# Attention scores from two float32r parts on opposite halves of the array, in place of three bfloat16 parts on one

## What is computed

```python
xn = layernorm(x)                                  # x: 1024 x 512
q = rope(xn @ wq + bq)                             # 32 heads of 16
k = rope(xn @ wk + bk); v = xn @ wv + bv           # 8 key/value heads, each used by 4 heads
s = softmax(q @ k.T / sqrt(16)) @ v                # per head, 1024 x 1024 scores
z = xn @ W.T + b; m = sum_e p[e] * (xn @ A[e]) @ B[e]
g = silu(z + minimum(0.5 * norm(z) / (norm(m) + 1e-6), 1) * m)
out = x + s * g
```

## Time and profile before

| what | value |
|---|---|
| median of 3 runs | 495.08 us (494.57 to 496.36) |
| span of the profiled execution, first to last instruction | 494.9 us |
| opening part, to the first transposed scores | 104.2 us |
| groups 1 to 6, each | 47.34 us |
| TensorE / VectorE / ScalarE / GpSimd busy | 477.9 / 373.0 / 308.8 / 92.2 us |

### The profile page before, as it was taken

How to read it: one execution, slowest core, us unless ns; L and a number is a source line. 1 busy time by engine, 2 the same in 40 slices (tenths; PEclk the granted TensorE clock), 3 DMA queues, 4 the chain that set the end, 5 groups by cost and what they waited for, 6 DMA issues and landing times.

```text
span 494.9 us, 8174 instructions
## 1 busy us (share of the span) xinstructions
PE 477.9 (97%) x2437; PEld 166.2 (34%) x2437; DVE 373.0 (75%) x401; ACT 308.8 (62%) x603; POOL 92.2 (19%) x160
## 2 busy tenths in 40 slices
PE   7995999999999999999999999999999999999994
PEld 3772444432333332333232323232333323333231
DVE  5643898989888888888888888888888888833433
ACT  2221112377767777767777776767676777766774
POOL 4573225550000010001000100010001001001553
PEclk9997999999999999999999999999999999999999
DMA  8899965550000000000000000000000000002010
GB/s 302 263 119 117 116 79 64 64 66 1 2 0 3 2 1 1 1 0 1 0 1 0 1 0 1 0 1 0 1 0 1 0 1 1 0 2 75 19 49 29
DMA packets 16980, 17.06 MB, mean 34 GB/s; under 512 B 3394, under 2 KB 14914, under 8 KB 16962
## 3 DMA queue, kind: packets, MB, share of 16 engines
q1 hardware_dynamic: 15332, 15.21, 18.3%
q10 hardware_dynamic: 1632, 1.64, 1.0%
HBM read 6.76 MB, written 2.10 MB: 18 GB/s over the span
## 4 chain that ended last, share of the span: by engine, by line
PE 83%; DVE 4%; DMA 4%; POOL 3%; ACT 2%; issue 2%; SPq 1%; DVEq 0%
PE oT L839 26%; PE sm L777 24%; PE st L875 23%; PE sm L857 3%; DMA kA<-arena 2%; PE oT L720 2%; PE st L720 2%; DMA x_sb<-in_x 1%; PE sm L848 1%; POOL arena L315 1%; ACT arena L526 1%; DVE arena L577 1%; DVE arena L575 1%; DVE arena L573 1%; PE sm L860 1%
## 5 line engine op out<-in xcount | busy, mean ns | idle before, releaser
L595 DVE TENSOR_REDUCE negmax<-sm 128x1 f32<-128x1024 f32 x256 | 303.8, 1220 | 63.0 <-PE sm L777 62.4
L526 ACT ACTIVATE arena<-st 128x512 f32<-128x512 f32 x512 | 268.1, 601 | 99.0 <-PE st L875 98.2
L777 PE MATMUL sm<-kA,qA 96*128 (+1 forms) x512 | 155.1, 384 | 7.0 <-DMA kA<-arena 5.3
L875 PE MATMUL st<-qA,kA 98*128 (+1 forms) x512 | 158.4, 380 | 1.6 <-ACT arena L526 1.4
L839 PE MATMUL oT<-arena,vg 128*32 128x512 f32 x1024 | 136.4, 605 | 0.7 <-ACT arena L526 0.7
L777 PEld LDWEIGHTS sm<-kA,qA 96*128 (+1 forms) x512 | 39.5, 97 | 149.0 <-issue 117.8
L875 PEld LDWEIGHTS st<-qA,kA 98*128 (+1 forms) x512 | 49.1, 97 | 92.2 <-ACT arena L526 41.4
L361 POOL TENSOR_TENSOR maxp<-negmax,consts 128x16 bf16<-128x16 f32 x16 | 3.4, 215 | 261.9 <-PE st L875 210.6
L839 PEld LDWEIGHTS oT<-arena,vg 128*32 128x32 f32 x1024 | 20.1, 108 | 37.2 <-issue 24.8
L451 ACT ACTIVATE arena<-arena 128x512 bf16<-128x512 f32 x10 | 6.3, 630 | 40.8 <-POOL arena L315 40.8
L674 DVE TENSOR_TENSOR xT_sb<-sm,b_sb 128x512 f32<-128x512 f32 x4 | 2.8, 692 | 21.1 <-PE sm L860 21.1
(11 more groups left out here) (88 smaller groups left out, 255.0 us busy)
## 6 DMA issues: line engine op xcount, KB each, us to landing
qA<-arena SPq DMA_DIRECT2D x48, 128.0 KB, 5.4
x_sb<-in_x SPq DMA_DIRECT2D x8, 256.0 KB, 6.5
kA<-arena SPq DMA_DIRECT2D x12, 128.0 KB, 6.6
wT_sb<-in_wT SPq DMA_DIRECT2D x1, 1024.0 KB, 8.0
out<-x_sb SPq DMA_DIRECT2D x1, 896.0 KB, 4.0
out<-x_sb SPq DMA_DIRECT2D x4, 224.0 KB, 2.0
arena<-in_wq SPq DMA_DIRECT2D x1, 768.0 KB, 11.1
arena<-in_cosT ACTq DMA_DIRECT2D x1, 512.0 KB, 7.4
```

Of the source, the lines that this page charges most:

```text
L526: act.activation(probs[:, s % PB, h, :], st[:, (st_score(0, s, h) - late) % 3, :], ACT.Exp, scale=float(D) ** -0.5).then_inc(st_free, 1)
L595: dve.tensor_reduce(negmax[:, half, r:r + 1], sm[:, bank, :], AX.X, ALU.max, negate=True).then_inc(sm_free, 1)
L777: mm = pe.matmul(sm[:, bank, kh * HALF:(kh + 1) * HALF], qA[0:KR, half, bass.ds(g, 1), h, qt * P:(qt + 1) * P] .rearrange("p a n -> p (a n)"),
L875: pe.matmul(st[:, (st_score(0, s, h) - fewer) % 3, :], kA[:, bass.ds(g, 1), kt * P:(kt + 1) * P].rearrange("p a n -> p (a n)"), qA[:, half ...
```

## The change

q and k are split into two float32r parts (a high part, and what is left), three products of 16 rows: 48 partitions, 50 with the maxima. Even groups use partitions 0 to 49, odd groups 64 to 113 of `qA` and `kA`, which are now four-byte tiles. So row scores of group g+1 and transposed scores of group g lie in opposite halves of the array's rows, and `step` issues them in turn. Values moved behind the second of four pairs; in the last group the late pieces stand together behind the values. `turn_heads` stands ahead of the slot's first transposed scores. To put even and odd groups 64 partitions apart, the columns of wq (GpSimd, `put_columns`, from a landing place in `z_sb`), of wk (TensorE, every other column, two matmuls of 64 output rows) and the rows of the rope tables and biases (DMAs by halves, `load_tables`) are laid out anew. The rows of ones are a memset of all of `kA` on GpSimd instead of a DMA. Row entries of group 0 come two at a time behind every second matmul of a projection. TensorE's and SP's loops over groups are unrolled. Cut to its core:

```diff
-PARTS = 3
-Q_SLOTS = (0, 1, 0, 1, 0, 2)
-K_SLOTS = (0, 0, 1, 1, 2, 0)
+PARTS, PART_BUFS = 2, 3
+Q_SLOTS = (0, 0, 1)
+K_SLOTS = (0, 1, 0)
+ROWS = 64
+SLOT_DMAS = 2 * len(Q_SLOTS)
-PARTNER = [i ^ 8 for i in range(32)]
+PARTNER = [i ^ 4 for i in range(32)]
...
-        qA = sb("qA", [KM, 2, KV, REP, HALF], BF16)
-        kA = sb("kA", [KM, KV, S], BF16)
+        qA = sb("qA", [P, 2, KV // 2, REP, HALF], F32R)
+        kA = sb("kA", [P, KV // 2, S], F32R)
-        maxT = sb("maxT", [32, 2, P], BF16)
+        maxT = sb("maxT", [32, 2, P], F32R)
...
+        wq_came = z_sb[:, :, :].rearrange("p c (k d a h) -> p k a c d h", k=CHUNKS, a=2, h=REP)
+        wq_rows = wq_sb.rearrange("p c (k a d h) -> p k a c d h", k=CHUNKS, a=2, h=REP)
...
+        def load_tables(queue, odd):
-            sp.dma_start(wq_sb[:, :, P:E], wq_v[:, :, P:E]).then_inc(wq_in, 16)
+            load_tables(sp, 1)
+            sp.dma_start(z_sb[:, :, P:E], wq_v[:, :, P:E]).then_inc(wq_in, 16)
-            sp.dma_start(kA[KR:KM, :, :], ones).then_inc(ones_in, 16)
+            load_tables(act, 0)
...
                     maxima_row(0, 0)
                 of_slot = K_SLOTS if kind == "k" else Q_SLOTS
+                    sp.wait_ge((part1, part2)[of_slot[slot]], n + 1)
+                    for odd in range(2):
...
+                        sp.dma_start(to.bitcast(F32),
+                                     parts[odd * ROWS:(odd + 1) * ROWS, n % PART_BUFS, of_slot[slot], :]
+                                     ).then_inc(stacked[n], 16)
...
+            pool.memset(kA[:, :, :].bitcast(F32), 1.0).then_inc(ones_set, 1)
             pool.wait_ge(const_set, 6)
+
+            def put_columns(k):
+                for odd in range(2):
+                    pool.tensor_copy(wq_rows[:, k, odd], wq_came[:, k, odd]).then_inc(wq_put, 1)
 
             for t in range(NT):
                 pool.wait_ge(mean_var, t + 1)
                 pool.tensor_scalar(mv[:, t, 1:2], mv[:, t, 1:2], EPS_LN, None, ALU.add).then_inc(eps_added, 1)
                 pool.wait_ge(eps_added, t + 1)
                 pool.tensor_tensor(rstd[:, t:t + 1], mv[:, t, 1:2], consts[:, 0:1], ALU.pow).then_inc(rstd_done, 1)
+                if t == TH:
+                    pool.wait_ge(wq0_in, 16)
+                    put_columns(0)
+            pool.wait_ge(wq_in, 16)
+            for k in range(1, CHUNKS):
+                put_columns(k)
...
-            def left_over(n):
+            def low_part(n):
                 pool.wait_ge(part1, n + 1)
-                pool.tensor_tensor(rot[:, n % 2, :], rot[:, n % 2, :], parts[:, n % 3, 0, :],
-                                   ALU.subtract).then_inc(left1, 1)
-
-            def third_part(n):
-                pool.wait_ge(part2, n + 1)
-                pool.tensor_tensor(parts[:, n % 3, 2, :], rot[:, n % 2, :], parts[:, n % 3, 1, :],
-                                   ALU.subtract).then_inc(part3, 1)
+                pool.tensor_tensor(parts[:, n % PART_BUFS, 1, :].bitcast(F32R), rot[:, n % 2, :],
+                                   parts[:, n % PART_BUFS, 0, :], ALU.subtract).then_inc(part2, 1)
...
-                    if c < rows:
-                        next_maximum()
+                    if c % 2 == 1:
+                        for _ in range(max(0, min(2, rows - (c - 1)))):
+                            next_maximum()
...
+                            for odd in range(2):
+                                mm = pe.matmul(pj(n)[odd * ROWS:(odd + 1) * ROWS, tok], wk_sb[:, c, odd::2],
+                                               xT[:, i, c, tok], start=(c == 0), stop=(c == NE - 1))
...
-                if freed is not None:
-                    pe.wait_ge(sm_free, freed)
-                for kh in range(2):
+                rows = slice(ROWS * (g % 2), ROWS * (g % 2) + KR)
+                for kh in halves_of_keys:
+                    if kh == 0 and freed is not None:
+                        pe.wait_ge(sm_free, freed)
                     mm = pe.matmul(sm[:, bank, kh * HALF:(kh + 1) * HALF],
-                                   qA[0:KR, half, bass.ds(g, 1), h, qt * P:(qt + 1) * P]
-                                   .rearrange("p a n -> p (a n)"),
-                                   kA[0:KR, bass.ds(g, 1), kh * HALF:(kh + 1) * HALF].rearrange("p a n -> p (a n)"),
-                                   start=True, stop=True)
-                mm.then_inc(sm_full, 1)
+                                   qA[rows, half, g // 2, h, qt * P:(qt + 1) * P],
+                                   kA[rows, g // 2, kh * HALF:(kh + 1) * HALF], start=True, stop=True)
+                    if kh == 1:
+                        mm.then_inc(sm_full, 1)
...
                         pe.matmul(st[:, (st_score(0, s, h) - fewer) % 3, :],
-                                  kA[:, bass.ds(g, 1), kt * P:(kt + 1) * P].rearrange("p a n -> p (a n)"),
-                                  qA[:, half, bass.ds(g, 1), h, :].rearrange("p a n -> p (a n)"),
+                                  kA[rows, g // 2, kt * P:(kt + 1) * P], qA[rows, half, g // 2, h, :],
                                   start=True, stop=True).then_inc(st_full, 1)
 
-                    def next_rows(e):
+                    def next_rows(e, kh):
                         if not last:
                             n = sm_score(g, e, first)
-                            score_rows(g + 1, e, n, sm_score(0, e, first) % 2, n - 1)
+                            score_rows(g + 1, e, sm_score(0, e, first) % 2, n - 1, (kh,))
...
-                    score_cols(0)
                     if s == OUT1_SLOT and not first:
                         n = SM_LAST["out1"] if last else sm_out1(g)
                         turn_heads(1, (n if last else sm_out1(0)) % 2, 2 * g, n - 1)
                     if s == OUT0_SLOT:
                         n = SM_LAST["out0"] if last else sm_out0(g)
                         turn_heads(0, (n if last else sm_out0(0)) % 2, 2 * g + 1, n - 1)
-                    if last:
-                        units = list(LATE_UNITS.get(s, ()))
+                    score_cols(0)
+                    next_rows(2 * s, 0)
                     score_cols(1)
-                    next_rows(2 * s)
-                    if last and units:
-                        late_unit(*units.pop(0))
-                    score_cols(2)
+                    next_rows(2 * s, 1)
                     if s > 0:
                         values(g, s - 1, st_score(g, s - 1, 3) + 1 - (1 if last and s - 1 >= MAX0_SLOT else 0),
                                None if first and s == 1 else 2 * g + (s - 1) // NT)
                     elif not first:
                         values(g - 1, 15, st_score(g - 1, 15, 3) + 1, None)
-                    if last and units:
-                        late_unit(*units.pop(0))
-                    next_rows(2 * s + 1)
+                    if last:
+                        for unit in LATE_UNITS.get(s, ()):
+                            late_unit(*unit)
+                    score_cols(2)
+                    next_rows(2 * s + 1, 0)
                     score_cols(3)
-                    if last and units:
-                        late_unit(*units.pop(0))
+                    next_rows(2 * s + 1, 1)
 
             step(0, first=True)
             for n in range(len(halves) - 2, len(halves)):
-                pe.wait_ge(stacked[n], 16 * len(Q_SLOTS))
-            with pe.Fori(1, LAST) as g:
+                pe.wait_ge(stacked[n], 16 * SLOT_DMAS)
+            for g in range(1, LAST):
                 step(g)
             step(LAST, last=True)
             values(LAST, 15, st_score(LAST, 15, 3), None)

```

More of the change, by code:

```diff
@@ L25 @@
 BF16 = mybir.dt.bfloat16
+F32R = mybir.dt.float32r
 ACT = mybir.ActivationFunctionType
@@ L145, in build @@
         parts_at = NE * E + 2 * S + 4 * HALF
-        parts = arena[:, parts_at:parts_at + n_parts].bitcast(BF16).rearrange(
-            "p (b k n) -> p b k n", b=3, k=PARTS)
+        parts = arena[:, parts_at:parts_at + n_parts].rearrange(
+            "p (b k n) -> p b k n", b=PART_BUFS, k=PARTS)
         cos_sb, sin_sb = tables[:, 0, :], tables[:, 1, :]
@@ L227, in build @@
         LATE = (KV - 1) * REP * D
+        def load_tables(queue, odd):
+            rows = slice(odd * ROWS, (odd + 1) * ROWS)
+            queue.dma_start(bias[rows, 0:CHUNKS, :], biases[:, 0:CHUNKS, :]
+                            .rearrange("(d a h) c k -> a d h c k", a=2, h=REP)[odd]).then_inc(small_in, 16)
+            queue.dma_start(bias[rows, CHUNKS, :], biases[:, CHUNKS, :]
+                            .rearrange("(d h a) k -> a d h k", a=2, h=REP)[odd]).then_inc(small_in, 16)
+            for to, table in ((cos_sb, cosT), (sin_sb, sinT)):
+                queue.dma_start(to[rows, :],
+                                table.rearrange("(d a h) n -> a d h n", a=2, h=REP)[odd]).then_inc(tab_in, 16)
         block = ctx.enter_context(nc.Block())
@@ L272, in step @@
                 maxima_row(g, 1)
-                if more:
+                if g < LAST:
```

(4 more changed lines are left out.)

85 lines of the change are left out of this document (35 added, 50 removed).

## The result

| | before | after |
|---|---|---|
| median of the runs shown together | 495.48 us | 502.86 us (501.13 to 505.66, 4 runs) |
| span of the profiled execution | 494.9 us | 501.7 us |

A forecast was written before the change was run, and what follows sets the result against it. TensorE bounds the kernel, issuing without a hole in 2.83 us slots; afterwards an exp wait sets 2.57. 494.9 + 1.0 (opening) - 1.8 (group 0) - 20.9 (groups 1 to 6) + 9.4 (last) = 482.6 span, median 482.8; range 474 to 506.

The forecast's parts named there:

- The wait that sets the slot: Slot after the change: next values wait for the exp of the fourth transposed score, 2.57 us from values to values.
- the 0.42 from c2 to the start of its exp: In a slot: c2, third of four transposed scores c0 to c3, starts at 1.00 us, its exp at 1.42.
- the row entries in twos at 0: Opening part: issuing group 0's row entries two at a time is the same work and costs 0.
- the passage from a late piece to the scores at 0.1: Last group: the first piece behind values costs 0.1 us extra, 11 times, within the +9.4 us.
- (a): Rival: halves do not run side by side, a pair costs 0.43 us, groups keep their time; 505 us, chance 0.18.
- (b): Rival: each change between halves costs some 0.12 us, eight a slot and no overlap, slot 3.79; 612 us, chance 0.03.
- (c): Rival: float32r streams at half speed with overlap, a pair costs 0.43 us, slot 2.80; 521 us, chance 0.06.
- The loop over c1 and the three banks: In a slot: c1, the second transposed score, waits for the exp of c2; a shorter loop, 2.39 us to values.
- (e): Rival: the exp loop does not bind, VectorE's 2.36 us does, 0.2 less in 112 slots; 460 us, chance 0.03.
- Group 0: First group: 43.3 us from slots and extras, plus 1.8 for four VectorE gate operations, against 46.92; -1.8 us.
- The last group: No row scores, late pieces no longer cover the exps, slots of 2.57: 60.7 us against 51.3, so +9.4.
- (d): Rival: forecast holds and k1 stacking goes by pieces, not bytes, first maximum some 5 us earlier; 476 us, chance 0.14.

The follow-up runs named there:

- run 9: Kernel before, with values cut into two pieces of two heads, behind the third and fourth transposed scores, and copies of `oT` moved ahead of exps: 622.9 us.
- run 5: Changed kernel with values two slots behind their scores instead of one, copies of `oT` and turned heads one slot later: 506.29 us (ratio 1.0221).
- run 2: Changed kernel with the last group alone in its old order, late pieces between transposed scores and values behind the third: 500.53 us (ratio 1.0086).
- run 4: Changed kernel with one row entry of group 0 behind each projection matmul instead of two behind every second one: 519.0 us, one time.
- run 3: On top of run 2, all other groups in their old order too, on the new layout with opposite halves: 515.14 us (ratio 1.0409).
- run 1: Changed kernel with row scores reading the same half as the transposed scores of their pair, so maxima are wrong: 698.8 us, one time.
- run 11: On run 2: `oT` copied before the third transposed score's exp, a slot's late pieces together before that score, `idb_sb` load first: 496.41 us (ratio 1.0007).

## Why the prediction was wrong

The wait that sets the slot was named rightly. Three terms failed: the 0.42 from c2 to the start of its exp (measured 0.53), the row entries in twos at 0 (a visit to the halves costs 0.41 to 0.43), and the passage from a late piece to the scores at 0.1 (0.19).

- **Price of a score matmul: right.** 0.22 to 0.23, in float32r, side by side in opposite halves. Rivals (a), (b) and (c) are out. The result lies near (a)'s 505 us by accident: there the groups keep their time, and here they gained 11.5 us with group 0. (The slot of (b) adds up to 3.81, not 3.79.)
- **A slot: the right loop, one term too small.** The step "exp of c2 starts at 1.42" took 0.42 from the earlier trace rows, from a score whose load went ahead beneath another matmul. Behind values the load is bare and the step is 0.53 (run 9: 0.51 for bfloat16). That is 0.1 in 16 slots, 1.6 us a group. The slot with the turned heads is 3.74 (250.09 to 253.83 on the timeline), 1.07 more in place of 0.88, and the copy of `oT` costs 0.49 as forecast. A group is 45.8 (274.7 / 6) in place of 43.9: 11.2 us over six groups, the largest miss.
- **The next bound: half said.** The loop over c1 and the three banks stood in the prediction as 2.39, with the same 0.42 and with 0.31 to values; with bare loads at both places it is 2.61 (run 5). No order tried here gets below it, and VectorE's 2.36 (rival (e)) was never near.
- **Group 0: right by luck.** -1.5 over the stretch of the forecast, -1.8. Its slots are 2.67 as elsewhere (129.80 to 132.47), 1.6 too much, but the four gate operations on VectorE, taken at 1.8, cost some 0.3: two slots of 2.80, the others 2.67. The two misses cancel.
- **The last group: right sum of terms, two of them too small, and the cause in part another.** A slot was taken at 2.57 and is 2.67, 1.6 us in 16. The first piece behind values was taken at 0.1 beyond its 0.86 and costs 0.19 (a slot with two pieces is 4.58, with one 3.73), 1.0 us in 11; the rest of the 3.0 lies at the turned maxima and heads. The prediction called the cause the lost cover of the exps. Only 3.1 us go when the pieces stand between the scores again (run 2); 8.8 stay, and they come with bare loads and passages between 50 and 128 rows, 0.64 in a slot with two pieces.
- **The opening part: a cost taken as 0.** "Row entries in twos are the same work: 0" failed. A visit costs 0.41 to 0.43 (run 4), and there are 19 of them, 8 us; from the first row maximum to values the stretch grew by 4.5 (from 62.6 to 67.1). Of the difference at most 1.7 is the half clock, which lasted 3.4 us in place of 6.8; some visits may lie in waits for VectorE, which was not measured. Stacking by bytes was right (k1 landed 10.10 after 35.07, as 10.12 before), so rival (d) fell. (Its 18 DMAs in 22.30 us are 1.24 each, not 1.12 to 1.2.) The first rope waited 1.9 longer, and that was covered.
- **The tail** was costed at 0 and took 1.2: values of the last slot ran at half clock (1.98 in place of 1.11).
- The misses add up: 11.2 (groups) + 3.0 (last group) + 3.7 (opening) + 1.2 (tail) = 19.1 us, the distance from the forecast span of 482.6 to 501.7. (The forecast's stretches of group 0 and of the last group overlap by one slot, which matters little.) The 3.7 and the 1.2 hold differences between executions too, as the starts of values from 113.5 to 115.3 show. No rival had the change of tiling as a cost outside the groups.

## What to carry to other kernels

Packing two matmuls into opposite halves of the array works and gives back nearly the whole of one, but price the passages between that layout and matmuls that use the array otherwise: some 0.4 us for going in and out once. Read a latency from a row in the same position, since the first matmul behind such a passage, or behind a wait, also shows its weight load. When work changes its place in an order, compare the two orders between points that hold the same work. And when TensorE's work shrinks, write out the next loop with every bank in it before believing that the engine's sum sets the slot.

## What the runs showed of the hardware that was not expected

- No weight load went ahead of a passage to another tiling: in the profiles of before, of the changed kernel and of run 2, load and matmul start within 0.03 us of each other there, where both are recorded, where a load of the same tiling went up to 0.43 ahead (458.48 and 458.91 before). The Trainium skill (TensorE: Matmul & The Clock Gate, Step-by-step: what each phase is for) says that loads are pulled ahead of running matmuls where rows don't conflict or the spare weight buffer is the target; the rows before agree, and those of run 2 show where it stops.
- A matmul in one half started ahead of one in the other half that stands before it in the program (run 3: c3 at 266.69, r3 at 267.02), and the exp that waited for it started 0.79 behind it in place of 0.53.
- A granted clock of 0.5 for 355 us with TensorE busy 29.8 of 30 us ahead of it (run 1), in one execution.
- Stretches of half clock vary from profile to profile: 3.4 to 10.2 us between 42 and 59 us, 17.1 us from 123.3 in run 4, and times vary with the clock. Run 11 spread from 493.57 us (mean granted clock 0.993) to 499.90 us (0.983) over 12 runs.
